# Cross-attention 0 of a twelve-part decoder: where the row maxima are put, and who takes them for the first pair of heads

## The reference

```
qw = (q_in @ Wq + bq).reshape(B, M, HEADS, QSIZE)
kw = (k_in @ Wk + bk).reshape(B, N, HEADS, QSIZE)
vw = (v_in @ Wv + bv).reshape(B, N, HEADS, KSIZE)
a = jnp.einsum('bmhd,bnhd->bhmn', qw, kw) / jnp.sqrt(jnp.float32(QSIZE))
a = jnp.where(key_mask[:, None, None, :], a, -jnp.inf)
a = jax.nn.softmax(a, axis=-1)
o = jnp.einsum('bhmn,bnhd->bmhd', a, vw).reshape(B, M, HEADS * KSIZE)
return o @ Wo + bo
```

## Time and profile before

| | us |
|---|---|
| median of three runs | 6297.54 (6292.7 to 6310.4) |
| profiled execution | 6303.64 |
| its span in the trace | 6301.9 |
| PE busy in the span | 5355.4 (85%) |
| ACT, DVE and POOL busy | 3078.9, 2960.6, 2202.3 |

### The profile page before, as it was taken

The page is one execution under the profiler, slowest core; times in us unless marked ns, Lnnn a source line. Parts: engine busy times, 40 slices in busy tenths (PEclk is TensorE's granted clock), DMA queues, the critical chain, the costliest instruction groups (busy, mean ns, idle before and its releaser), DMA issues. The chain is left out here.

```text
span 6301.9 us, 68800 instructions
## 1 busy us (share of the span) xinstructions
PE 5355.4 (85%) x27758; PEld 1700.8 (27%) x27772; DVE 2960.6 (47%) x3378; ACT 3078.9 (49%) x3081; POOL 2202.3 (35%) x1100
## 2 busy tenths in 40 slices
PE   6758999999999999979897499997973688888879
PEld 2213333333333333332342211111431111111123
DVE  6575454544545452025622500001156999988613
ACT  3214545445444445521122299997121277777842
POOL 1006888888887889915442000000000000000000
PEclk7758999999999999989998799998886699999979
DMA  1000000000000000010000200000003000000001
GB/s 41 14 0 1 1 1 1 1 1 1 1 1 1 1 1 1 1 39 1 2 0 9 95 25 18 18 1 8 19 23 125 11 10 10 10 10 11 2 19 34
DMA packets 64812, 89.14 MB, mean 14 GB/s; under 512 B 9791, under 2 KB 49780, under 8 KB 62894
## 3 DMA queue, kind: packets, MB, share of 16 engines
q1 hardware_dynamic: 64494, 84.73, 4.2%
HBM read 59.33 MB, written 25.38 MB: 13 GB/s over the span
## 5 line engine op out<-in xcount | busy, mean ns | idle before, releaser
L2405 DVE TENSOR_REDUCE red<-ps 128x2 f32<-128x1024 f32 (+1 forms) x832 | 978.0, 1185 | 1003.7 <-PE ps L2223 1000.5
L2342 ACT ACTIVATE Pr<-ps,key_bias 128x1024 f32<-128x1024 f32 x816 | 897.6, 1114 | 1049.2 <-PE ps L2238 1048.3
L2455 POOL TENSOR_TENSOR Ps<-Ps,Pr 128x1024 f32<-128x1024 f32 x400 | 942.7, 2357 | 279.9 <-ACT Pr L2342 279.9
L2891 DVE TENSOR_REDUCE red<-ps 128x2 f32<-128x1024 f32 (+2 forms) x1102 | 961.7, 926 | 80.9 <-PE ps L2806 67.6
L2464 POOL TENSOR_TENSOR Ps<-Ps,Pr 128x1024 f32<-128x1024 f32 x400 | 946.6, 2366 | 0.0
L2869 ACT ACTIVATE Pr<-ps 128x1024 f32<-128x1024 f32 x816 | 786.2, 1021 | 226.4 <-PE ps L2816 225.4
L492 POOL MEMSET sel<- 16x2048 f32 (+1 forms) x2 | 2.7, 1368 | 2430.0 <-POOLq L89 2430.0
L2236 PE MATMUL ps<-Q,Kr 64*128 64x512 f32 x3264 | 840.9, 593 | 0.0
L2255 PE MATMUL ps<-Pr,Vc 128*64 128x512 f32 x3264 | 789.7, 605 | 0.0
L2994 ACT ACTIVATE Pr<-ps 128x2048 f32<-128x2048 f32 x467 | 726.2, 2025 | 1.6 <-PE ps L2960 1.6
L2806 PE MATMUL ps<-Kp,Q 52*128 52x512 bf16 (+1 forms) x1664 | 450.4, 411 | 224.8 <-DVE red L2891 148.9
(11 more groups left out here) (561 smaller groups left out, 5102.7 us busy)
## 6 DMA issues: line engine op xcount, KB each, us to landing
L_dram_K<-parts SPq DMA_DIRECT2D x26, 384.0 KB, 2.7
Kp<-L_dram_K SPq DMA_DIRECT2D x16, 624.0 KB
L_dram_K<-parts SPq DMA_DIRECT2D x26, 256.0 KB, 2.2
Kp<-L_dram_K SPq DMA_DIRECT2D x16, 416.0 KB
w<-L_ffn_experts_w_dram SPq DMA_DIRECT2D x24, 256.0 KB, 3.1
ctx<-ctx_dram SPq DMA_DIRECT2D x13, 256.0 KB, 5.5
L_dram_K<-parts SPq DMA_DIRECT2D x26, 128.0 KB, 1.7
keep<-L_dram_mask SPq DMA_DIRECT2D x13, 256.0 KB, 3.7
```

The costliest lines, as they stand in the source:

```text
L2342: nc.scalar.activation(Pr[:, t % 4, half].rearrange("p a n -> p (a n)"), ps[:, 2 * half:2 * half + 2, :].rearrange("p a n -> p (a n)"), AC ...
L2405: nc.vector.tensor_reduce(red[:, g // C % 2, q, :, g % C], ps[:, maxima_bank(g, q):maxima_bank(g, q) + 2, 0:ctx.keys_in(g % C)], AX, ALU.m ...
L2455: nc.gpsimd.tensor_tensor(into, into, src, ALU.add).then_inc(*summed0.up())
L2891: nc.vector.tensor_reduce(red_flat[:, g % 2, first:first + n], ps[:, b:b + n, 0:ctx.keys_in(g % C)], AX, ALU.max).then_inc(*reduced.up())
```

## The change

Two things change in `cross_0`.

First, in turns from g = 14 on, the last maximum of a step that is step 0, has another item, or has three maxima, goes into banks 0 and 1 in place of 4 and 5, and is issued behind the scores, the projections and the other item, ahead of the products. It waits there for the exponential that reads the first half of the scores, and the next tile's first scores wait for its reduction.

Second, for the first pair of heads (turns 0 to 12), five of the eight items of each chunk (q = 0, 2, 4, 5, 7) are no longer reduced from PSUM by VectorE. ScalarE copies the two banks to SBUF in bf16 (`moved`, three slots), which frees the banks, and VectorE takes a running maximum by column of bf16 against bf16 (`kept`). Behind the 13th chunk five reductions of `kept` over 1024 columns each bring these into `red`. `kept` and the first pair's half of `red` are filled with -3e38 ahead of the loops. The two tiles lie where `Pr` lies later.

```diff
-    def maxima_bank(i, q):
-        return (4, 0, 2)[(8 * i + q) % 3] if i < LAG else 4
+    by_act = (0, 2, 4, 5, 7)
+    with ExitStack() as early:
+        kept, moved = k.tile(early, "kept", [128, len(by_act), 2, CHUNK], BF16), k.tile(early, "moved", [128, 3, 2, CHUNK], BF16)
...
+    def maxima_bank(g, s, steps, q):
+        items = maxima_at(g, s, steps)
+        if g < LAG:
+            return (4, 0, 2)[(8 * g + q) % 3]
+        return 0 if q == items[-1] and len(items) > 1 and (s == 0 or others_at(g, s) or len(items) > 2) else 4
...
-            take_banks(b, reduced.at(8 * i + q + 1))
+            take_banks(b, copied.at(len(by_act) * i + by_act.index(q) + 1) if i < C and q in by_act else reduced.at(8 * i + q + 1))
...
-                between = 2 if s == 0 or others else 1
+                last = [q for q in items[1:] if g >= LAG and maxima_bank(g, s, steps, q) == 0]
+                between = [q for q in items[1:] if q not in last]
                 for q in items[:1]:
-                    maxima(g, q)
+                    maxima(g, s, steps, q)
                 if 0 <= j < N:
                     scores(j, s, 0)
-                for q in items[1:between]:
-                    maxima(g, q)
+                if s == 0 or others or g < LAG:
+                    for q in between:
+                        maxima(g, s, steps, q)
                 if 0 <= j < N:
                     scores(j, s, 1)
-                for q in items[max(1, between):]:
-                    maxima(g, q)
                 if s == 0:
                     keys_and_values(g + 1, j + 1)
+                elif not others and g >= LAG:
+                    for q in between:
+                        maxima(g, s, steps, q)
                 for item, p in others:
-                    item(p)
+                    {"queries": queries, "rows": rows, "sums": sums, "output": output}[item](p)
+                for q in last:
+                    maxima(g, s, steps, q)
                 if 0 <= j and 0 < t <= KT * P and (j < N or s == 0):
                     products(t - 1)
...
+                for q in maxima_at(g, s, steps) if g < C else ():
+                    if q in by_act:
+                        m, n, b = len(by_act) * g + by_act.index(q), ctx.keys_in(g), maxima_bank(g, s, steps, q)
+                        nc.scalar.wait_ge(*maxima_mm.at(8 * g + q + 1))
+                        if m >= 3:
+                            nc.scalar.wait_ge(*reduced.at(8 * ((m - 3) // len(by_act)) + by_act[(m - 3) % len(by_act)] + 1))
+                        nc.scalar.copy(moved[:, m % 3, :, 0:n], ps[:, b:b + 2, 0:n]).then_inc(*copied.up())
...
+        nc.vector.memset(red[:, 0], -3e38).then_inc(*folding.up())
+        nc.vector.memset(kept[:], -3e38).then_inc(*folding.up())
+        nc.vector.wait_ge(*folding.at(2))
...
+                    if g < C and q in by_act:
+                        m, n = len(by_act) * g + by_act.index(q), ctx.keys_in(g)
+                        nc.vector.wait_ge(*copied.at(m + 1))
...
+                        into = kept[:, by_act.index(q), :, 0:n]
+                        nc.vector.tensor_tensor(into, into, moved[:, m % 3, :, 0:n], ALU.max).then_inc(*reduced.up())
+                        continue
...
+                for n, q in enumerate(by_act if p == 0 else ()):
+                    nc.vector.tensor_reduce(red[:, 0, q, :, 0], kept[:, n], AX, ALU.max).then_inc(*folding.up())
+                if p == 0:
+                    nc.vector.wait_ge(*folding.at(2 + len(by_act)))
```

More of the change, by code:

```diff
@@ L2167, in cross_0 @@
         "summed0", "summed1", "inverse_step", "x_added")
+    folding, copied = k("folding", "maxima_copied")
     wq, wk, wv = (k.load(stack, weights, n, io["L0_xattn_" + n]) for n in ("Wq", "Wk", "Wv"))
@@ L2196, in maxima_at, with others_at @@
         return range(8 * s // steps, 8 * (s + 1) // steps) if 0 <= g < N else range(0)
-    def maxima_bank(i, q):
-        return (4, 0, 2)[(8 * i + q) % 3] if i < LAG else 4
+    def others_at(g, s):
+        return [(item, p) for item, p in ((item, pair_for(g, s, turn, step)) for item, turn, step in
+                (("queries", -1, 1), ("rows", C, 1), ("sums", LAG + C, 1), ("output", LAG + C + 2, 2))) if p is not None]
+    def maxima_bank(g, s, steps, q):
[3 more added lines that the diff above has]
+        return 0 if q == items[-1] and len(items) > 1 and (s == 0 or others_at(g, s) or len(items) > 2) else 4
     def pair_for(g, s, turn, step):
@@ L2213, in take_banks, with maxima @@
             taken[b] = when_free
-        def maxima(i, q):
-            b = maxima_bank(i, q)
-            take_banks(b, reduced.at(8 * i + q + 1))
+        def maxima(i, s, steps, q):
+            b = maxima_bank(i, s, steps, q)
+            take_banks(b, copied.at(len(by_act) * i + by_act.index(q) + 1) if i < C and q in by_act else reduced.at(8 * i + q + 1))
             if q == 0:
@@ L2309, in pe @@
                 t = KT * (j // C) + TPC * (j % C) + s
-                items = maxima_at(g, s, steps)
-                others = [(item, pair_for(g, s, turn, step)) for item, turn, step in
-                          ((queries, -1, 1), (rows, C, 1), (sums, LAG + C, 1), (output, LAG + C + 2, 2)) if pair_for(g, s, turn, step) is not None]
-                between = 2 if s == 0 or others else 1
+                items = list(maxima_at(g, s, steps))
+                others = others_at(g, s)
+                last = [q for q in items[1:] if g >= LAG and maxima_bank(g, s, steps, q) == 0]
+                between = [q for q in items[1:] if q not in last]
                 for q in items[:1]:
-                    maxima(g, q)
+                    maxima(g, s, steps, q)
                 if 0 <= j < N:
                     scores(j, s, 0)
-                for q in items[1:between]:
-                    maxima(g, q)
+                if s == 0 or others or g < LAG:
+                    for q in between:
+                        maxima(g, s, steps, q)
                 if 0 <= j < N:
                     scores(j, s, 1)
-                for q in items[max(1, between):]:
-                    maxima(g, q)
                 if s == 0:
                     keys_and_values(g + 1, j + 1)
+                elif not others and g >= LAG:
+                    for q in between:
+                        maxima(g, s, steps, q)
                 for item, p in others:
-                    item(p)
+                    {"queries": queries, "rows": rows, "sums": sums, "output": output}[item](p)
+                for q in last:
+                    maxima(g, s, steps, q)
                 if 0 <= j and 0 < t <= KT * P and (j < N or s == 0):
@@ L2401, in dve @@
                 for q in maxima_at(g, s, steps):
+                    if g < C and q in by_act:
+                        m, n = len(by_act) * g + by_act.index(q), ctx.keys_in(g)
+                        nc.vector.wait_ge(*copied.at(m + 1))
+                        if g:
+                            nc.vector.wait_ge(*reduced.at(8 * (g - 1) + q + 1))
+                        into = kept[:, by_act.index(q), :, 0:n]
+                        nc.vector.tensor_tensor(into, into, moved[:, m % 3, :, 0:n], ALU.max).then_inc(*reduced.up())
+                        continue
                     nc.vector.wait_ge(*maxima_mm.at(8 * g + q + 1))
@@ L2404, in dve @@
                         nc.vector.wait_ge(*rows_step.at(3 * (g // C) - 4))
-                    nc.vector.tensor_reduce(red[:, g // C % 2, q, :, g % C], ps[:, maxima_bank(g, q):maxima_bank(g, q) + 2, 0:ctx.keys_in(g % C)], AX, ALU.max).then_inc(*reduced.up())
+                    nc.vector.tensor_reduce(red[:, g // C % 2, q, :, g % C], ps[:, maxima_bank(g, s, steps, q):maxima_bank(g, s, steps, q) + 2, 0:ctx.keys_in(g % C)], AX, ALU.max).then_inc(*reduced.up())
                 p = pair_for(g, s, -1, 1)
```

## The result

| us | before | after |
|---|---|---|
| median of 4 runs each, same chip | 6297.16 | 6222.57 (6218.11 to 6228.74) |
| ratio, 95% interval | | 0.9878 [0.9864, 0.9892] |
| profiled execution | 6303.64 | 6219.88 |
| its span | 6301.9 | 6218.1 |

The forecast was 6222.5. That it was met to 0.1 us is luck: four executions of one kernel lie some 10 to 18 us apart, by the interval the gain lies between 68 and 86 us, and two errors in the terms partly cancel. So the terms are checked one by one. Stages are cut at four events, always the same ones: the first memset that the change may follow (`mz`), the first key projection, the first scores, the last maximum.

A forecast was written before the change was run, and what follows sets the result against it. TensorE was taken to set the pace of the 90 turns, GpSimd next at 85%. Gains of 66 us there and 9 in the prologue made 75: 6303.6 to 6228.6, or 6222.5 on the median's scale, range 6204 to 6250.

The forecast's parts named there:

- GpSimd takes nothing back: 90 turns: GpSimd's 1628 us of additions fit into the shortened 1855 us, 88% busy; its tail keeps its length.
- both waits for `red` go: Step 0 of ordinary turns: waits of 0.42 and 0.32 us vanish, and the next scores keep 0.6 us of slack.
- steady term: Gain over the 90 turns: 66 us in all, 0.6 us per ordinary turn, possibly 0.45 to 0.75.
- the 0.1 charged: Step 0: 0.1 us for an added operand change ahead of the moved maximum; the step ends at 6.71, or 6.61 without.
- The running maximum at 0.69: Prologue: VectorE's bf16 maximum of 1024 columns takes 0.69 us, as the cast into bf16 does.
- The rival with 1.226: Prologue: the bf16 maximum takes 1.226 us, so the prologue costs 16 us and the kernel takes 6248; chance 12%.
- A chunk of 10.0: Prologue: a chain of 9.2, 9.6 or 11.2 us in turn, mean 10.0 against 11.3, 1.3 less per chunk.
- The fold, 5.7: End of prologue: five reductions of `kept`, 1024 columns at 1.14 us each, add 5.7 us once.
- The memset, 0.8: Ahead of the prologue: filling `kept` takes 4.3 us plus 0.2 for `red`; after 3.73 us of idle, 0.8 is left.
- The warmer clock: Prologue: TensorE's clock goes up, taking with shorter maxima about 1 us more off each chunk, 6211 us; chance 8%.
- Half of the gain: 90 turns: bare loads and the maximum's wait for the exponential cost 0.3 us a turn, 6256 us; chance 8%.
- The slower case: 90 turns: a late moved reduction stops the next scores, slower from 1.2 us late, 6360 us at 2; chance 3%.

The follow-up runs named there:

- e5: `after` with a reciprocal of 320 columns on VectorE ahead of the moved maximum's reduction in step 0 of all 90 turns: 6351.56 us.
- e1: `after` with the moved maxima alone, the first pair's maxima all reduced by VectorE from PSUM as before: 6222.69 us, ratio 0.9882.
- e6: `after` with ScalarE's copies and the running maximum kept in f32 in place of bf16: 6244.13 us.
- e9: e8 with ScalarE copying items 0, 1, 4, 5, 6 of each chunk in place of 0, 2, 4, 5, 7: 6203.68 us, ratio 0.9843.
- e10: e8 with ScalarE copying items 2, 3, 4, 5, 6 of each chunk in place of 0, 2, 4, 5, 7: 6230.15 us.
- e8: `after` with GpSimd filling `kept` and `red`, and three bf16 maxima of halves ahead of the fold's reductions: 6215.92 us, ratio 0.9869.

## Why the prediction was right, and where its terms were off

*TensorE sets the pace of the 90 turns, and GpSimd takes nothing back.* Right. TensorE is busy 1837.5 of 1847.5 us and the tail kept its length (245.8 in both).

*Step 0: both waits for `red` go, no new one comes.* Right, as the timeline shows; over the 90 turns the view of waits has this for the scores, in total, times, longest:

```profile
PEld ps L2250 <- DVE red L2441: 0.5, 1, 0.5
...
PE ps L2250 <- DVE red L2441: 0.2, 1, 0.2
```

The view leaves out the small one: behind the two reductions in a row of a three-tile turn the scores start 0.21 late, where 0.15 was forecast. The slack in ordinary turns was forecast at 0.6 and is 0.76 by the timeline, 0.66 by e5.

*The size of the steady term.* This is the term that was mis-sized: 66 us forecast, 74.3 measured (73.4 in e1). Ordinary turns gained 0.64, not 0.6: the 0.1 charged for one more change of row groups (from 128-row operands to 64-row ones) is not in the trace. From the value projection to what follows it is 0.99 us with the maximum there (977.12 to 978.11), and it was 0.99 with the products there (to 1010.88 in the earlier trace rows):

```profile
1009.89 1.05 PE L2267 MATMUL ps<-Wv,ctx 128*128 128x128 f32 x8
```

The 1.95 us that the prediction took for both projections end where the next operation starts, so they held already what this change costs, and the 0.1 came on top. The forecast of 6.61 "without the charge" is the measured step to the hundredth. The Trainium skill ("TensorE: Matmul & The Clock Gate", section "Step-by-step: what each phase is for") has a load pulled ahead if the row groups don't conflict, or if it goes into the background weight buffer; the prediction used the first condition alone. It worked out a gain of 0.53 a turn from this, and 0.64 came; no run shows which of the two conditions holds behind the value projection.

By kind of turn, from first maximum to first maximum in both traces:

| turns | forecast, us each | measured, us each |
|---|---|---|
| 63 ordinary, from the second turn on | 0.6 | 0.64 |
| 6 of three tiles | 3.1 | 3.69 |
| 6 with `sums` | 1.1 | 0.96 |
| 6 with `output` | 1.1 | 1.37 |
| 6 with the short chunk | -0.65 | -0.40 |

The first turn and the last two make up the rest (+0.4). A turn of three tiles went from 21.35 to 17.66. The second and third step are right to 0.1, but its first step was 7.65 before, not the 7.25 of an ordinary one, since VectorE was late with `mz` there and the second maximum waited longer. The lateness is that of one small operation, of 16 columns, beside an addition on GpSimd. Before:

```profile
1045.95 2.36 POOL L2455 TENSOR_TENSOR Ps<-Ps,Pr 128x1024 f32<-128x1024 f32 x1
...
1047.09 1.31 DVE L2440 TENSOR_TENSOR mz<-neg,mz 128x16 bf16<-128x16 f32 x1
```

and the same operation in `after` behind the first pair, where GpSimd is idle:

```profile
487.22 0.23 DVE L2480 TENSOR_TENSOR mz<-neg,mz 128x16 bf16<-128x16 f32 x1
```

The prediction read only the second and third step of this turn. After the change the operation still takes 1.30 us there, but nothing waits for it, and the first step is 6.61.

*The running maximum at 0.69.* Right: 686 ns. The trace agrees with the double rate that the Trainium skill gives bf16 `tensor_tensor` from SBUF ("VectorE: DVE Perf Modes", section "The perf-mode tier table"), and e6 with its f32 column: a factor of 1.78. Some 0.14 us doesn't depend on the columns: 520 of them take 0.42 in bf16 and 0.685 in f32, so that each further column takes 0.53 and 1.06 ns, a factor of 2.0 (estimates from these rows). The rival with 1.226 falls, and e6 shows what it would have cost: 11.9 us a chunk, where the prediction's walk gave 12.1.

*A chunk of 10.0.* Right in mean and as a mechanism: 10.08, and e9 against e10 shows that it is a chain and not a load. The prediction's walk has the projection wait for the user of its banks, item 7, 0 or 1 in turn, and the three lengths 9.06, 10.06 and 11.12 come in that rotation, where it had 9.2, 9.6 and 11.2. The gain a chunk is 1.2, not 1.3, and the first chunk gained nothing (11.51 and 11.56): from the first to the 13th key projection it is 12.5 us, where 15.6 was forecast.

*The fold, 5.7.* Measured 5.72, though the prologue behind the 13th projection grew by 4.0 only, as the short last chunk gained 2.0. *The memset, 0.8.* Mis-sized: 1.9, for the 1.0 us of idle time ahead of it. This idle time could be read in the trace of before: the two memsets of 8192 columns in the earlier trace rows have 3.5 us of it, 1.76 each, and two of 4096 columns have 0.9 each:

```profile
L2684 DVE MEMSET Q<- 2x4096 uint32 x2 | 6.9, 3472 | 1.8 <-issue 0.9 <-DVE Q L2681 0.9
```

The prediction scaled the 6.885 us of the row alone. With the idle time, 5120/8192 of 8.65 are 5.4 us; `after` has 1.01 + 4.33 = 5.3, and the term would have come out at 1.9. In all the prologue's part brought 8.5 - 1.9 = 6.6 where 9 was forecast. So the steady term was 8.3 us too small and this one 2.5 too large: -81 by the stages, where -75 was forecast.

*The rivals.* The warmer clock fell: 0.55 before and 0.56 after in the prologue, projections still 2.07 us. "Half of the gain" fell with e1. The slower case is real from 1.3 us of delay on (e5), and nothing in `after` comes near it in ordinary turns.

## What to carry to other kernels

Where the engine that sets the pace waits for banks, look for banks that another stream leaves idle at that moment, and count how long they stay so: here 1.7 us of use fitted into a gap that had 0.7 to spare, and the same move without the other banks cost 0.5 us a turn. When work is shared between two engines that feed a third in order, it isn't enough to alternate them: `after` alternates more (0, 2, 4, 5, 7 on ScalarE) than e9 (0, 1, 4, 5, 6), which is 1.0 us a chunk faster. Give each item to the engine that is free when the item comes, here items 2 and 3 to VectorE while ScalarE is held by the key copies. The choice among the same eight items moved the time by 27 us, more than the split itself had brought. And a detour over SBUF pays by its type: in bf16 it won 8.5 us of the prologue, in f32 it lost 13.5, with 1.9 us for the fill on top in both.

## What the hardware showed that was not expected

- The row of a large memset on VectorE does not hold all of its price. 5120 columns are a row of 4.33 us in bf16 (`after`) and in f32 (e6), with 1.01 and 1.02 us of idle time ahead that no wait explains. Over the traces this idle time grows with the columns, 0.9, 1.0 and 1.76 us ahead of 4096, 5120 and 8192, and there is next to none ahead of the 512 of `mz`. Idle time and row together are 1.07, 1.04 and 1.06 ns a column. Why it shows as idle time stays open.
- An operation of VectorE with two inputs in SBUF waits for GpSimd. The 16 columns of `mz<-neg,mz` take 0.23 us where GpSimd is idle and 1.30 to 1.32 at the six next pair borders, before and after, and there they end 0.09 us behind the end of GpSimd's addition (1045.95 + 2.36 = 1048.31, and 1047.09 + 1.31 = 1048.40). The running maximum of 520 columns shows the same: 0.41 to 0.43 us alone, but 1.26 for the one of the two below that started 0.2 us behind the start of GpSimd's cast of `Qb`, in `after` and in e8; the other had started before the cast and took 0.42. The Trainium skill ("SBUF — State Buffer", section "Who interferes with whom") has a VectorE instruction with two SBUF inputs and a GpSimd instruction that reads SBUF exclude each other, whoever comes first; the traces agree. No experiment was made on it.

```profile
478.20 1.60 DVE L2436 TENSOR_TENSOR kept<-kept,moved 128x520 bf16<-128x520 bf16 x2
...
478.35 1.17 POOL L2510 CAST Qb<-Q 128x1024 bf16<-128x1024 f32 x1 [132.63 <-DVE Q L2448]
```

- TensorE's granted clock between 360 and 470 us, which lies in the prologue of every kernel, was 0.50 to 0.56: 0.55 before, 0.50 in e1, 0.55 and 0.52 in the two traces of `after`, 0.56 in e9, with TensorE busy 61, 64, 66, 67 and 70 of 110 us. The shorter chunks did not bring the higher level.
